# Another order of the fillers in layer 1's attention: maxima between feed-forward pieces, one down product and an output norm a batch later

## The reference, cut to what matters

```python
# x: (4, 512, 256), 16 heads of 16
qkv = x @ W_qkv.T + b_qkv                       # causal, per head
a = softmax(where(causal, -inf, q @ k.T / 4)) @ v
x = layernorm(x + a @ W_out.T + b_out)
w_up, w_down = dequant4bit(...).T + lora_a @ lora_b
x = layernorm(x + relu(x @ w_up + b_up) @ w_down + b_down)     # 256 -> 1024 -> 256
```

## Time and profile before

| | us |
|---|---|
| median of 3 runs | 853.78 |
| lowest, highest | 853.75, 856.44 |
| span of the profiled execution | 851.4 |
| median less that span | 2.4 |

### The profile page before, as it was taken

One profiled execution on the slowest core, in us unless ns is written; L12 is line 12 of the kernel. 1 busy time (PEld: TensorE's weight loads), 2 busy tenths in 40 slices (PEclk: granted clock), 3 DMA queues, 4 the chain that ended last, 5 costly groups with the idle time before them and its releaser, 6 DMA issues. The chain is left out here.

```text
span 851.4 us, 11512 instructions
## 1 busy us (share of the span) xinstructions
PE 767.9 (90%) x3907; PEld 409.4 (48%) x3908; DVE 446.6 (52%) x1198; ACT 359.7 (42%) x565; POOL 115.4 (14%) x127
## 2 busy tenths in 40 slices
PE   5599999999999999999997879888998989989886
PEld 3222444444435556666665445434464445533675
DVE  2744554565435622222247676868765674662453
ACT  3389775685684012212223233444423442156030
POOL 0000000000000311111842411231011110022000
PEclk9699999999999999999999899989999999999999
DMA  7567207005107161111125870006300370000000
GB/s 217 148 204 223 93 26 209 27 25 149 38 26 247 43 198 46 43 45 46 32 84 169 251 201 2 1 27 187 110 1 3 106 216 1 2 1 26 14 12 26
DMA packets 51582, 75.01 MB, mean 88 GB/s; under 512 B 7607, under 2 KB 44763, under 8 KB 49227
## 3 DMA queue, kind: packets, MB, share of 16 engines
q1 hardware_dynamic: 49660, 69.26, 27.0%
q0 software_dynamic: 1872, 5.11, 2.2%
HBM read 46.57 MB, written 27.66 MB: 87 GB/s over the span
## 5 line engine op out<-in xcount | busy, mean ns | idle before, releaser
L656 PE MATMUL ps<-arena 128*128 128x256 f32 (+3 forms) x1084 | 326.7, 450 | 18.2 <-issue 2.9
L656 PEld LDWEIGHTS ps<-arena 128*128 128x128 f32 x1084 | 201.2, 195 | 106.6 <-issue 68.7
L970 ACT ACTIVATE arena<-ps 128x1024 f32<-128x1024 f32 x128 | 124.2, 1027 | 32.9 <-PE ps L711 32.6
L1067 ACT ACTIVATE arena<-ps 128x1024 f32<-128x1024 f32 (+3 forms) x128 | 82.9, 702 | 114.1 <-PE ps L903 114.0
L1450 DVE TENSOR_REDUCE arena<-ps 128x1 f32<-128x512 f32 (+3 forms) x176 | 100.4, 633 | 28.5 <-PE ps L881 27.6
L769 PE MATMUL ps<-arena 128*128 x184 | 86.5, 593 | 0.6 <-DVE arena L1177 0.6
L711 PE MATMUL ps<-arena 96*128 96x512 bf16 x256 | 71.4, 390 | 7.0 <-DMA arena<-q_stacks_dram 3.9
L1565 POOL TENSOR_SCALAR_AFFINE_SELECT arena<-arena 128x512 f32<-128x512 f32 x64 | 41.7, 652 | 253.3 <-ACT arena L1067 253.3
L725 PE MATMUL ps<-arena 128*32 128x512 f32 x512 | 69.6, 611 | 2.9 <-DVE arena L1223 2.7
L879 PE MATMUL ps<-arena 96*128 96x128 bf16 (+3 forms) x256 | 62.3, 303 | 9.6 <-DVE arena L1450 5.7
L648 PE MATMUL ps<-arena 128*128 128x128 f32 (+3 forms) x237 | 38.6, 302 | 23.3 <-DVE arena L1216 10.5
(11 more groups left out here) (153 smaller groups left out, 678.4 us busy)
## 6 DMA issues: line engine op xcount, KB each, us to landing
arena<-stacks_dram SPq DMA_DIRECT2D x16, 768.0 KB, 5.9
arena<-in_gate_up_proj SPq DMA_DIRECT2D x8, 1024.0 KB, 9.3
arena<-q_stacks_dram SPq DMA_DIRECT2D x8, 768.0 KB, 5.8
stacks_dram<-arena SPq DMA_DIRECT2D x16, 384.0 KB, 3.3
arena<-in_down_proj SPq DMA_DIRECT2D x8, 512.0 KB, 8.7
stacks_dram<-arena SPq DMA_DIRECT2D x16, 256.0 KB, 3.3
q_stacks_dram<-arena SPq DMA_DIRECT2D x8, 384.0 KB, 4.1
yg_dram<-arena SPq DMA_DIRECT2D x23, 128.0 KB, 1.7
```

What stands on the lines that cost most here:

```text
L656: last = nc.tensor.matmul(dst[0:rows, lo:hi], a, w, start=(n == 0), stop=(n == len(pairs) - 1))
L970: nc.scalar.activation(probs[:, 2 * p:2 * p + 2, :], ps[:, 2 * p:2 * p + 2, :], ACT.Exp)\
L1067: nc.scalar.activation(cprobs[:, i % 2, 2 * p:2 * p + 2, P * kt:S], ps[:, 2 * p:2 * p + 2, P * kt:S], ACT.Exp).then_inc(exp_done[p], 1)
```

## The change

Four strings get another order, and the gather for batch 3 is issued at another step. In the second and third string (batches 1 and 2) both cX stand in slot 0, cQ0 ahead of cP0, and cV0 and cV1 beside cF0. The maxima come from slot 6 on, mostly three and then a cH or a cD, instead of behind the cHs and twelve in slot 13. cD0 to cD2 are in slots 12 to 14, cD3 in slot 3 of the next batch, and cM comes behind cD1. In the third string cO0 and cO1 come behind cK3 in slot 6, ahead of the first maximum. In the fourth, cD3 of batch 1 fills slot 3, cO0 and cO1 come behind cN, slots 13 and 14 have no filler, and slot 15 has cD1. At the end cD3 of batch 2 comes ahead of cP1, cO0 of batch 2 behind cN1, cO1 behind cI8, and cD1 of batch 3 behind cI15. The steps are the same ones, the same number of times. Layer 0 and batch 0's slots are as before.

```diff
-C_SECOND = """-cF3 +cX0 | -cP0 +cX1 +cQ0 | +cK0 -cP1 +cQ1 | +cK1 +cQ2 | .cF0 +cQ3 +cK2 =cO0 +cK3 | +cV0 +cV1 =cO1
-| -cN0 -cN1 -cH0 -cH1 >cL0 | -cH2 -cH3 >cL1 >cE0 +m +m +m +m -cH4 +m +m | .cF1 -cH5 +m +m -cH6 +m +m +m
--cH7 +m | +m +m +m | +m +m +m -cD0 +m +m +m | +m +m -cD1 +m +m +m +m | .cF2 +m +m +m -cD2 +m +m | +m
-+m +m +m +m +m +m +m +m +m +m +m | +cm0 +cM0 -cD3 |  |"""
+C_SECOND = """-cF3 +cX0 +cX1 | +cQ0 -cP0 | +cK0 -cP1 +cQ1 | =cD3 +cK1 +cQ2 | .cF0 +cV0 +cK2 +cV1 | +cQ3 -cN0 >cL0
+| -cN1 -cH0 +cK3 >cL1 >cE0 =cO0 =cO1 +m +m +m | -cH1 +m +m +m -cH2 +m +m +m | .cF1 +m +m +m -cH3 +m +m +m
+| -cH4 +m +m +m -cH5 +m +m +m | +m +m +m -cH6 +m +m +m | +m +m +m -cH7 +m +m +m +m
+| .cF2 +m +m +m -cD0 +m +m +m +m | +m +m +m +cm0 -cD1 +cM0 | -cD2 | |"""
...
-C_LAST = """-cF3 | -cP0 | -cP1 | =cO0 | .cF0 =cO1 -cN0 -cN1 | -cH0 -cH1 | -cH2 | -cH3 | .cF1 -cH4 | -cH5 |  |
--cH6 | .cF2 -cH7 | -cD0 | -cD1 | -cO0 |"""
-C_END = """-cF3 =cD2 -cP0 -cP1 =cD3 -cN0 -cI0 -cI1 -cI2 -cI3 -cI4 -cN1 -cI5 -cI6 -cI7 =cO1 -cI8 -cI9
--cI10 -cI11 -cD0 -cI12 -cI13 -cD1 -cI14 -cI15 -cO0 -cD2 -cD3 -cO1"""
+C_LAST = """-cF3 | -cP0 | -cP1 | =cD3 | .cF0 -cN0 -cN1 =cO0 | -cH0 -cH1 =cO1 | -cH2 | -cH3 | .cF1 -cH4 | -cH5 | -cH6 |
+-cH7 | .cF2 -cD0 | | | -cD1 |"""
+C_END = """-cF3 =cD2 -cP0 =cD3 -cP1 -cN0 -cI0 -cI1 -cI2 -cI3 -cI4 -cN1 =cO0 -cI5 -cI6 -cI7 -cI8 =cO1 -cI9
+-cI10 -cI11 -cD0 -cI12 -cI13 -cI14 -cI15 -cD1 -cO0 -cD2 -cD3 -cO1"""
...
-                if n == "cL" and i == 1 and 1 <= b < B - 1:
-
-                    pool.wait_ge(x2_ready, 2 if b == 1 else 2 * b + 2)
-                    gather(b + 1)
+                if n == "cL" and i == 1 and b == 1:
+
+                    pool.wait_ge(x2_ready, 2)
+                    gather(2)
+                if n == "cP" and i == 1 and b == 0:
+
+                    pool.wait_ge(x2_ready, 2 * B - 2)
+                    gather(B - 1)
```

More of the change, by code:

```diff
@@ L85 @@
 | +m +m +m +m | .cF1 +m +m | +m +m +m +m | +m +m +m +m | +m +m +m +m +m | .cF2 +m +m +m +m | +cm0 +cM0 | >cL0 | >cL1 >cE0 |"""
-C_SECOND = """-cF3 +cX0 | -cP0 +cX1 +cQ0 | +cK0 -cP1 +cQ1 | +cK1 +cQ2 | .cF0 +cQ3 +cK2 =cO0 +cK3 | +cV0 +cV1 =cO1
-| -cN0 -cN1 -cH0 -cH1 >cL0 | -cH2 -cH3 >cL1 >cE0 +m +m +m +m -cH4 +m +m | .cF1 -cH5 +m +m -cH6 +m +m +m
--cH7 +m | +m +m +m | +m +m +m -cD0 +m +m +m | +m +m -cD1 +m +m +m +m | .cF2 +m +m +m -cD2 +m +m | +m
-+m +m +m +m +m +m +m +m +m +m +m | +cm0 +cM0 -cD3 |  |"""
[L90 to L93, removed]
-C_LAST = """-cF3 | -cP0 | -cP1 | =cO0 | .cF0 =cO1 -cN0 -cN1 | -cH0 -cH1 | -cH2 | -cH3 | .cF1 -cH4 | -cH5 |  |
--cH6 | .cF2 -cH7 | -cD0 | -cD1 | -cO0 |"""
-C_END = """-cF3 =cD2 -cP0 -cP1 =cD3 -cN0 -cI0 -cI1 -cI2 -cI3 -cI4 -cN1 -cI5 -cI6 -cI7 =cO1 -cI8 -cI9
--cI10 -cI11 -cD0 -cI12 -cI13 -cD1 -cI14 -cI15 -cO0 -cD2 -cD3 -cO1"""
+C_SECOND = """-cF3 +cX0 +cX1 | +cQ0 -cP0 | +cK0 -cP1 +cQ1 | =cD3 +cK1 +cQ2 | .cF0 +cV0 +cK2 +cV1 | +cQ3 -cN0 >cL0
+| -cN1 -cH0 +cK3 >cL1 >cE0 =cO0 =cO1 +m +m +m | -cH1 +m +m +m -cH2 +m +m +m | .cF1 +m +m +m -cH3 +m +m +m
+| -cH4 +m +m +m -cH5 +m +m +m | +m +m +m -cH6 +m +m +m | +m +m +m -cH7 +m +m +m +m
+| .cF2 +m +m +m -cD0 +m +m +m +m | +m +m +m +cm0 -cD1 +cM0 | -cD2 | |"""
+C_THIRD = """-cF3 +cX0 +cX1 | +cQ0 -cP0 | +cK0 -cP1 +cQ1 | =cD3 +cK1 +cQ2 | .cF0 +cV0 +cK2 +cV1 | +cQ3 -cN0 >cL0
+| -cN1 -cH0 +cK3 >cL1 >cE0 =cO0 =cO1 +m +m +m | -cH1 +m +m +m -cH2 +m +m +m | .cF1 +m +m +m -cH3 +m +m +m
+| -cH4 +m +m +m -cH5 +m +m +m | +m +m +m -cH6 +m +m +m | +m +m +m -cH7 +m +m +m +m
+| .cF2 +m +m +m -cD0 +m +m +m +m | +m +m +m +cm0 -cD1 +cM0 | -cD2 | |"""
+C_LAST = """-cF3 | -cP0 | -cP1 | =cD3 | .cF0 -cN0 -cN1 =cO0 | -cH0 -cH1 =cO1 | -cH2 | -cH3 | .cF1 -cH4 | -cH5 | -cH6 |
+-cH7 | .cF2 -cD0 | | | -cD1 |"""
+C_END = """-cF3 =cD2 -cP0 =cD3 -cP1 -cN0 -cI0 -cI1 -cI2 -cI3 -cI4 -cN1 =cO0 -cI5 -cI6 -cI7 -cI8 =cO1 -cI9
+-cI10 -cI11 -cD0 -cI12 -cI13 -cI14 -cI15 -cD1 -cO0 -cD2 -cD3 -cO1"""
 DVE_ONLY = ("rp", "rs", "re", "V", "F", "cF", "cK", "cL", "cE", "cm", "cO")
```

## The result

| | before | changed |
|---|---|---|
| median of 20 runs, us | 854.5 | 849.85 |
| lowest, highest | 852.56, 856.44 | 843.76, 855.14 |
| span of the profiled execution | 851.4 | 847.5 |
| that execution's own time | not given | 849.63 |

The ratio is 0.9942, with a 95% interval of 0.9927 to 0.9956: the changed kernel is 4.65 us faster by the medians. Its runs are spread over 11.4 us and those of before over 3.9. The forecast was 845.0, range 839.5 to 850.0; applied to the median of before, the interval is 848.3 to 850.7 us, so it lies across the upper bound of that range.

A forecast was written before the change was run, and what follows sets the result against it. With TensorE busy 90% and work unchanged, only PE's waits and half-clock time could be won. End -7.2, batch 3 -3.3, middle batches -1.6, clock +3.4 gave -8.7 from 853.8: 845 us, range 839.5 to 850.

The forecast's parts named there:

- (a): Program end: PE's waits for DVE and the half clock go by reordering cO0, cD3 and cD1; -7.2 us.
- (b): Batch 3: cD3 of batch 1 fills a 1.83 us wait, less the cost of slots without filler; -3.3 us.
- (c): Batches 1 and 2, what goes: small waits and the run of maxima at DVE's pace; -21.5 us in both.
- (d): Batches 1 and 2, what comes: waits of 3.8 and 2.7 us at second cH, +6.5; maxima and cH joints, +13.4.
- (e): Clock in batches 1 and 2: one drop behind each of the two long waits, +1.7 us each, +3.4 together.
- (f): Batch 3's gather issued behind cattS3's select on POOL: no effect on the time.
- the long drops: Rival: clock drops behind the middle batches' long waits last as long as at 561.9; 848.5 us, chance 0.07.
- The chain of joints from slot 7 to 13: Rival: DVE stays one group behind, so ten joints a batch pay 1.56 us each; +18, 863 us, chance 0.06.
- a swinging clock at the joints of the maxima: Rival: joints of slots 7 to 12 in two batches each bring a clock drop; +20, 865 us, chance 0.04.

The follow-up runs named there:

- e1: Kernel before with only the end's new order; median 847.41 us, ratio 0.9916.
- e8: Changed kernel with only cO0 and cO1 of batch 0 moved from slot 6 to behind cM0; median 845.18 us, ratio 0.9899.
- e4: Changed kernel with cL0, cL1, cE0 of batch 3 and cO0, cO1 of batch 0 moved to slot 13 behind cm0; 839.68 us, ratio 0.9837.
- e3: Kernel before with the new second and third strings, old tail, and cD3 of batch 1 in slot 3 of batch 3; 856.46 us, ratio 1.0032.
- e5: e4 with the gather for batch 3 back at its old step; median 840.97 us, ratio 0.9852.
- e10: Changed kernel with cH1 ahead of the first three maxima instead of behind them; median 845.31 us, ratio 0.9914.
- e9: e7 with seven maxima of slots 10 and 11 moved into slot 13 ahead of cm0; median 835.86 us, ratio 0.9780.
- e2: Kernel before with the new batch 3 and end; old middle except batch 2's cD2 moves to slot 14 and cD3 to batch 3; 845.76 us, ratio 0.9902.
- e7: e6 with cV1 ahead of cK2; median 831.46 us, ratio 0.9746.
- e6: e4 with cH3 and cD0 ahead of their slots' maxima, some maxima in fours, and cO0, cO1 behind cM0; median 833.53 us, ratio 0.9758.

## Why the prediction was right or wrong, point by point

The direction was right. The time was inside the range by 0.15 us, less than the interval's half width of 1.2, so that it was inside is luck. The gain was forecast at 8.7 us and measured at 4.65. The forecast was also taken from a median of three runs, 853.8; that of twenty is 0.7 higher.

- (a) The end: forecast -7.2, measured -7.1, in e1 alone as well. Each wait that was named went, cI0's 0.69 stayed as said, and the clock held.
- (b) Batch 3: forecast -3.3, measured -3.5. cattP14's wait for POOL is there, 0.48, and slot 14 lost 0.84 where 1.0 was forecast.
- (c) and (d), the small waits and the joints: forecast -21.5 and +13.4, so -8.1. Measured without the two long waits: batch 2 12.3 (e8) against 14.4, batch 1 19.3 less the 5.5 that slots 6 to 8 lost above e4's, 13.8, against 18.5: together -6.8. The parts that were named came: slot 8's 1.67 with the refill 1.83 (forecast 1.9), slot 12's 1.11 with it 1.27 (1.4), the third maximum 0.33 with it 0.50 (0.5). What I left out is max0's wait for the stacks in batch 1, 0.8: I had not asked what the earlier place of max0 would meet besides DVE.
- (d) and (e), the two long waits and the clock: the step that failed, by its size. Forecast +6.5 of wait and +3.4 of clock, 9.9. Measured 5.5 in batch 1 and 7.5 in batch 2, 13.0. The waits were 3.76 (forecast 3.8) and 3.52 (2.7). That the first agrees so well is in part luck: PE came to cH1@0 at 594.5, not 596, and DVE read max0 by 598, not 600. The drops were the larger miss. I gave each wait one drop at 1.7 us, as at the end. In batch 2 the first lasted 6.8 us, and a second came behind cH3's wait of 1.67, which I had priced as a plain wait. Batch 1 has the forecast 5.5 in this execution only; in e3 and e8, with its order, slots 6 to 8 lost another 2.1.
- (f) The gather: nothing, as e5 bears out within its scatter.

So the missing 4.0 us of gain are 3.1 in the long waits and their clock and 1.3 in the rest of the middle, less some tenths elsewhere.

Of the rivals, the long drops (848.5) came nearest. The chain of joints from slot 7 to 13 did not happen: behind slot 8 no wait for L1450 is above 1.11 us. Nor did a swinging clock at the joints of the maxima: in slots 9 to 13 of the changed kernel no stretch has the clock at 0.5. The Trainium skill, "TensorE: Matmul & The Clock Gate", section "A second HAM failure mode: psum-queue depth-cycling", says that short idling of PE while it goes round PSUM banks can make the clock swing. The stops of 0.2 to 0.4 us at the joints, and the one of 1.11 in slot 12, did not bear it out; behind a stop of 1.67 us, itself a wait for a bank, there was a drop in some executions (at 704.3 in the changed kernel, at 602.2 in e5) and none in others (e4).

The reason why the middle loses, stated in (d), is shown: the first maximum was placed behind a normalisation on DVE, three banks go round, and the third filler behind that maximum, the second cH, pays. Taking the normalisation away (e4), in one batch alone (e8) or giving PE one cH more ahead (e10) takes the wait away, in one batch, or down by what the cH is long, less what it costs on DVE. No run changed the number of banks; what speaks for the bank is that in e10 the wait moved to the filler that takes it. That the change's idea, the even spread, is good for 0.7 us a batch once this is out of the way is shown by e9's trace.

## What to carry to other kernels

A filler that is put early takes a bank early, and the wait shows at the third filler behind it, not at its own step; before you move work that one engine reads, ask what that engine has in its queue in front of it. Long vector work with no near deadline (here two norms) belongs behind the work that frees buffers, but a store that waits for it must not stand in a DMA queue ahead of something urgent. Where several orders are tried, sum the waits step by step in the trace: it told 0.7 us of order from 3 us of scatter, which the medians alone would not have.

## What the runs showed of the hardware that I had not expected

The price of a wait of PE is not a fixed number. The best case for this is one that the change does not touch. At the start of batch 1's attention PE waits 1.74 to 1.77 us for the maxima's DMA in all twelve traces. Behind it the clock was at 0.5 for 6.8 us in six of them (before, e1, e3, e5, e8, e9), for 3.4 in five (changed, e2, e4, e7, e10), and not at all in e6:

```profile
559.40 1.04 PE L903 MATMUL ps<-arena 98*128 98x512 bf16 x4 [1.77 <-DMA arena<-arena]
```

```profile
559.40:568.00 8.60, 7.79 (x47) 4.24 (x48) 4.13 (x12) 6.64 (x10) 1.90 (x3) 1.00 0.00 0
```

It is the same with the long waits. Three executions have the same order in batch 1 and waits of 3.4 to 3.8 us at the same step (the changed kernel, e3, e8). The clock was at 0.5 for 3.4, 10.2 and 10.2 us behind them, the 10.2 in two drops with the wait of 1.67 between them, and slots 6 to 8 of batch 1 lost 11.7, 13.7 and 13.8 us. Windows of e3:

```profile
597.70:604.50 6.80, 5.14 (x15) 2.61 (x15) 3.86 (x8) 0.69 (x1) 0.59 (x1) 0.50 0.78 195
611.30:614.70 3.40, 3.40 (x4) 1.23 (x5) 0.76 (x2) 0.00 (x0) 0.00 (x0) 0.50 0.00 0
```

In the 20 runs of the changed kernel the mean granted clock goes with the time (correlation -0.91). The five fastest, 843.8 to 846.8 us, have a clock of 0.971 to 0.973, the two slowest, 855.0 and 855.1, one of 0.961 and 0.962. In the kernel before it does too: -0.42 in the 17 runs beside e1 to e4, -0.81 and -0.83 in the two sets of 11. The changed kernel scatters more than it does (11.4 us against 3.9, 20 runs each), and e6 and e7 less than either (3.2 and 2.7, five runs each). That fits long waits with drops of changing length as the cause, but it is not shown: e9, without the long waits, scattered by 6.3 in five runs, and the kernel before by 7.2 in eleven. A single profile can mislead by some 4 us in one batch (19.3 against 23.3 in batch 1). What decides in a given execution whether a drop is short or long was not settled.
